# The bias of the last gate quarter moves from TensorE to VectorE in a quantised feed-forward stage

## What is computed

```python
def bit_linear(x, w, b):
    gamma_x = clip(max(abs(x), axis=-1), 1e-5)
    x_dq = clip(round(x * 127 / gamma_x), -128, 127) * gamma_x / 127
    gamma_w = clip(mean(abs(w)), 1e-5)
    w_dq = clip(round(w / gamma_w), -1, 1) * gamma_w
    return x_dq @ w_dq.T + b

gate = silu(bit_linear(x, gate_w, gate_b))     # 512 -> 2048
val = bit_linear(x, val_w, val_b)              # 512 -> 2048
x = x + bit_linear(gate * val, out_w, out_b)   # 2048 -> 512
```

## Time and profile before

| | us |
|---|---|
| median of 3 runs | 1772.95 |
| lowest and highest of them | 1772.92, 1774.59 |
| the profiled execution | 1772.19 |
| its span, first to last instruction | 1770.1 |
| the feed-forward stage in it | about 410 to 612 |
| granted TensorE clock, mean | 0.992 |

### The profile page before, as it was taken

One profiled execution on the slowest core, in us unless ns is written; L12 is line 12 of the kernel. 1 busy time (PEld: TensorE's weight loads), 2 busy tenths in 40 slices (PEclk: granted clock), 3 DMA queues, 4 the chain that ended last, 5 costly groups with the idle time before them and its releaser, 6 DMA issues. The chain is left out here.

```text
span 1770.1 us, 26445 instructions
## 1 busy us (share of the span) xinstructions
PE 1703.5 (96%) x9562; PEld 1391.0 (79%) x9582; DVE 1236.8 (70%) x2327; ACT 926.4 (52%) x1774; POOL 575.5 (33%) x455
## 2 busy tenths in 40 slices
PE   7999998997999979999999999999899999999998
PEld 6998997883444568888888788878777899999876
DVE  5444443796888768888788788888768576767555
ACT  4443332665565566666576667666331365656311
POOL 3111143014677532222222312121210355556332
PEclk9999999998999989999999999999999999999999
DMA  9323210963234671122222212110152579798563
GB/s 320 93 87 99 81 49 6 315 233 101 60 72 95 164 233 61 61 84 84 101 74 91 84 61 84 60 61 1 72 231 89 187 247 301 254 299 259 189 236 107
DMA packets 175563, 238.24 MB, mean 135 GB/s; under 512 B 51270, under 2 KB 112454, under 8 KB 173254
## 3 DMA queue, kind: packets, MB, share of 16 engines
q1 hardware_dynamic: 156620, 203.14, 35.1%
q0 software_dynamic: 9600, 33.30, 6.0%
q10 hardware_dynamic: 9216, 0.14, 0.3%
HBM read 184.24 MB, written 43.78 MB: 129 GB/s over the span
## 5 line engine op out<-in xcount | busy, mean ns | idle before, releaser
L1232 POOL TENSOR_TENSOR a_rq<-a_ssq,a_qhalf 128x4 f32<-128x4 f32 x64 | 65.6, 1025 | 358.8 <-DMA a_ssq<-a_sum_row 358.8
L78 PE MATMUL bank<-a_xT_hi,a_wq_lo 128*128 128x512 f32 (+1 forms) x384 | 144.3, 376 | 1.4 <-DVE a_xT_lo L503 1.4
L80 PE MATMUL bank<-a_xT_hi,a_wq_hi 128*128 128x512 f32 (+1 forms) x384 | 138.9, 362 | 0.0
L79 PE MATMUL bank<-a_xT_lo,a_wq_hi 128*128 128x512 f32 (+1 forms) x384 | 138.2, 360 | 0.0
L78 PE MATMUL bank<-a_wo_hi,a_oT_lo 128*128 128x512 f32 x320 | 127.3, 398 | 5.9 <-POOL a_wo_lo L1245 4.2
L1395 ACT ACTIVATE a_scores<-a_scores,a_nmax 128x256 f32<-128x256 f32 x256 | 126.9, 513 | 0.8 <-DVE a_nmax L1572 0.8
L80 PE MATMUL bank<-a_wo_hi,a_oT_hi 128*128 128x512 f32 x320 | 125.7, 393 | 0.0
L79 PE MATMUL bank<-a_wo_lo,a_oT_hi 128*128 128x512 f32 x320 | 125.7, 393 | 0.0
L2122 POOL TENSOR_TENSOR e_wg_lo<-raw_g,e_wg_hi 128x1408 fp32r<-128x1408 f32 x25 | 88.0, 3518 | 112.3 <-ACT e_wg_hi L2194 112.3
L1384 ACT ACTIVATE a_sum_row<-bank,a_sum_eps 1x512 f32<-1x512 f32 x64 | 43.4, 678 | 142.1 <-PE bank L1764 141.9
L1272 POOL TENSOR_TENSOR f_h<-f_vv,f_gs 128x512 f32<-128x512 f32 x64 | 92.8, 1454 | 61.4 <-DVE f_vv L1502 60.7
(11 more groups left out here) (423 smaller groups left out, 5380.1 us busy)
## 6 DMA issues: line engine op xcount, KB each, us to landing
raw_g<-in_egw SPq DMA_DIRECT2D x26, 704.0 KB, 4.5
raw_u<-in_euw SPq DMA_DIRECT2D x26, 704.0 KB, 6.0
a_xT_hi<-x1T_hi SPq DMA_DIRECT2D x16, 1024.0 KB, 6.2
a_xT_lo<-x1T_lo SPq DMA_DIRECT2D x16, 1024.0 KB, 8.3
raw_d<-in_edw SPq DMA_DIRECT2D x26, 512.0 KB, 3.9
y_routed<-m_y SPq DMA_DIRECT2D x39, 256.0 KB
raw_d<-in_edw SPq DMA_DIRECT2D x26, 192.0 KB, 4.4
a_cTraw<-in_ctxT SPq DMA_DIRECT2D x8, 512.0 KB, 5.7
```

What stands on the lines that cost most here:

```text
L78: pe.matmul(out, w[1], x[0], start=first, stop=False)
L79: pe.matmul(out, w[0], x[1], start=False, stop=False)
L80: return pe.matmul(out, w[0], x[0], start=False, stop=last)
L1232: pool.tensor_tensor(rq[:, h % HG, :], ssq[u % 2][:], qhalf[:], ALU.pow).then_inc(s_rq, 1)
```

## The change

For the last quarter of each tile (`j == NH - 1`) the bias product of TensorE is left out, and the first gate product opens the accumulation. VectorE takes the quarter out of its bank, scales it and adds the bias, in one instruction (`gate_biased`) that stands ahead of `val(n, 3)`, and writes it into `gs`. ScalarE then applies its function in place on `gs`, with no scale. The bias of this quarter, 512 numbers spread over 128 partitions (256 KB), is loaded once at the start of the stage, in front of the other transfers of SyncE. Two semaphores are new. The other three quarters are as before.

```diff
+        bg = sb("gate_bias", [P, 512])
...
+            sp.dma_start(bg[:], gate_bias_dram[H - 512:H].partition_broadcast(P)).then_inc(s_bg, 16)
             sp.dma_start(ahead.raw[:], wq_dram[:, :, 0:D]).then_inc(s_raw, 16)
...
             def silu(t, j):
                 u = t * NH + j
+                if j == NH - 1:
+                    act.wait_ge(s_gb, t + 1)
+                    act.activation(gs[u % 2][:], gs[u % 2][:], ACT.Silu).then_inc(s_gs, 1)
+                    return
                 act.wait_ge(s_g, u + 1)
...
+            def gate_biased(t):
+                u = t * NH + NH - 1
+                dve.wait_ge(s_g, u + 1)
+                dve.wait_ge(s_h, u - 1)
+                dve.scalar_tensor_tensor(gs[u % 2][:], gb[u % 2][:], sg[:, t:t + 1], bg[:], ALU.mult,
+                                         ALU.add).then_inc(s_gb, 1)
...
                     quantised_x(n + 3)
+                if n == 0:
+                    dve.wait_ge(s_bg, 16)
+                gate_biased(n)
                 val(n, 3)
...
-                    pe.matmul(gb[u % 2][:], rT[t % 3][:], gb6[:, cols], start=True, stop=False)
+                    if j < NH - 1:
+                        pe.matmul(gb[u % 2][:], rT[t % 3][:], gb6[:, cols], start=True, stop=False)
                     for c in range(KD):
-                        last = pe.matmul(gb[u % 2][:], xqT[t % 3][:, c, :], wg[:, c, cols], start=False, stop=c == KD - 1)
+                        last = pe.matmul(gb[u % 2][:], xqT[t % 3][:, c, :], wg[:, c, cols], start=c == 0 and j == NH - 1,
+                                         stop=c == KD - 1)
```

More of the change, by code:

```diff
@@ L1010, in ffn0_attention1 @@
 def ffn0_attention1(nc, banks, X, eps, ident, ones, limit, W, keep, prep, stored, rstd, x1T_dram, ahead, first, oT1,
-                    wq_dram, wo_dram, mask_dram, bq_dram, k_dram, v_dram, last, last_drams, B, S, G):
+                    wq_dram, wo_dram, mask_dram, bq_dram, k_dram, v_dram, last, last_drams, gate_bias_dram, B, S, G):
     T = B * S // P
@@ L1102, in ffn0_attention1 @@
         s_g, s_gs, s_v, s_vv, s_h = (sem(n) for n in ("gate", "silu", "val", "val_biased", "h"))
+        s_bg, s_gb = sem("gate_bias_loaded"), sem("gate_biased")
         s_half, s_ah, s_qh, s_sh, s_so, s_hr, s_hq = (sem(n) for n in (
@@ L2881, in program @@
                             k_dram, v_dram, last, (ktile(a["egw"][E]), ktile(a["euw"][E]), ktile(a["rwT"]), a["sdb"], a["egb"],
-                                                   a["eub"]), B, S, G)
+                                                   a["eub"]), a["gb"], B, S, G)
         if stop >= 4:
```

## The result

The changed kernel takes 1777.87 us (median of 10 runs, 1776.21 to 1783.17) against 1772.82 us for the kernel before (10 runs, 1770.14 to 1774.59). The ratio is 1.0032, with an interval of 1.0025 to 1.0040: 5.7 us slower (4.4 to 7.1). A second set of runs of the same kernel gave 1.0032 again (1.0021 to 1.0042). The prediction was 7.7 us slower, in a range that reaches from 2 to 13.

The account below looks back on a forecast made before the run. VectorE's loop with GpSimd and ScalarE was taken to bound most of the stage: sixteen rounds of 0.74 us, 11.8, less 4.1 absorbed, give 7.7 us on 1772.95, so 1780.7 us, range 1775.0 to 1786.0.

Parts of the forecast that it names:

- Who sets the pace: In most rounds VectorE's loop with GpSimd and ScalarE, not TensorE, whose sixteen removed products are worth 3.4 us if it bounds.
- the lag: Start of VectorE's last value quarter less start of TensorE's `down` products, same round; above some 3.5 us VectorE sets the pace.
- The rule from the Trainium skill: Improve the engine of highest occupancy: TensorE is the bound, so removing its products gives 3.4 us, 1769.5 us; chance 0.07.
- The step: VectorE's added instruction ahead of the last value quarter, 0.66 us each, sixteen times, 10.6 us in all.
- the 0.08 for ScalarE: Charge per round for ScalarE's later in-place function and its slower hand-over to GpSimd, 0.08 us (bounds 0 and 0.25).
- What absorbs: VectorE's waits for TensorE after round 0, nine of them, vanish when VectorE is late and take up 4.1 us.
- The reason that the prediction gave for the late rounds: In rounds 12 to 15 both paces are almost equal, VectorE 12.0 us and TensorE 11.8, so VectorE does not wait again.
- The sum: VectorE's last value quarter comes 11.8 - 4.1 = 7.7 us later, and attention starts later by the whole.
- the load: The 256 KB bias load at the stage's start takes 5.7 us, arrives before its first use and costs zero.
- One sign that was missed: The last value quarter of rounds 7 to 9 should move by 5 to 7 us, or the prediction is wrong.
- The passage into attention: At the stage's end TensorE is 5.5 to 6 us later with a lag near 3, and nothing is left to hide 2 us.
- ScalarE late: Its in-place function lasts 0.81 us or more and delays the norm and TensorE's `next_xT`; 11 us slower, 1784; chance 0.12.

Follow-up runs that it names:

- experiments 1: The changed kernel, but TensorE keeps its sixteen bias products of the last quarter; 1.0048 against the kernel before, 1.0035 when run again.
- 2: The kernel before, with the sixteen bias products of the last quarter left out and nothing in their place; 0.9990 against the kernel before.
- 5: The changed kernel with VectorE's new bias instruction done twice, the second over the first; 1.0104 against the kernel before.

## Why the prediction was right, point by point

**Who sets the pace: right.** The reading that rested on the waits and the lag held against the busy shares: 16 products removed from an engine that is 96% busy gave 1.5 us alone and 0.3 to 0.7 with the step there (experiments 1, 2), and a second step cost nearly in full (5). The rule from the Trainium skill, "Perfetto Trace Analysis", section "Identifying the Most-Contended Engine", which I had as a rival, named the wrong engine here when read by busy time alone: the edit takes work off the engine of highest occupancy, and the kernel is 5.7 us slower. The page's own warning is not to judge TensorE by that share but by its matmul throughput or its weight loads. Weight loads are busy 89.39 of 202 us in the stage, 44% against VectorE's 79%, so by that share the page does not point at TensorE.

**The step: 0.66 right, the 0.08 for ScalarE too much.** The rounds 0, 1, 2 and 4 to 11 grew by 0.66 to 0.73 us, 0.70 in the mean, not 0.74. Sixteen of them are 11.2 us, not 11.8. The in-place function lasts 0.63 us, under the 0.65 that I took and over the 0.61 estimated from the Trainium skill, "ScalarE: Activation LUTs", section "What ACT_TABLE_LOAD costs".

**What absorbs: right in place, small in size.** Rounds 3 and 12 to 15 took part of it up. From one last value quarter to the next, before and after:

| round | 3 | 12 | 13 | 14 | 15 |
|---|---|---|---|---|---|
| before | 13.11 | 12.02 | 11.64 | 12.13 | 11.66 |
| after | 13.00 | 11.93 | 11.43 | 11.42 | 11.44 |

They became 1.3 us shorter in place of 3.5 longer, which makes 4.85 absorbed, not 4.1. The waits alone are 4.1. What I left out is that a wait also breaks the overlap of two instructions: the next starts 0.65 us after a value quarter that lasts 0.74, but after a wait it starts only once the wait is over. That is some 0.09 us for each of nine waits. In the rows of after VectorE no longer waits in rounds 12 to 15, as the prediction asked. Its two waits left, both in round 0, are 2.9 us.

The reason that the prediction gave for the late rounds was only half right, though. It took both paces to be nearly equal there, 12.0 us for VectorE and 11.8 for TensorE. From tile 13 on there is no quantised input left to make, and VectorE's rounds 13 to 15 last 11.43 us, while the `down` products of rounds 12 to 14 stand 11.93 apart. So VectorE wins back 0.5 us in each of rounds 13 and 14, and the lag falls from 3.46 us in rounds 11 and 12 to 2.45 in round 14. It did not come to wait again because the lag was long enough for the few rounds left, not because the paces were equal.

**The sum.** 11.2 - 4.85 = 6.35 us at the last value quarter, and 6.5 at the stage's end, instead of 7.7. The timed 5.7 (4.4 to 7.1) agrees. The stated range, 2 to 13 us slower, is wide enough to hold almost any slower result, so these rows are the better test. Of the miss, 0.6 is the growth of a round and 0.75 the absorption. By the first measure the stage grew by only 5.5, because the second value quarter of round 0 came a microsecond earlier (8.04 us after the stage's start, where it was 9.05). Two executions of one kernel differ by 0.8 us there, with the clock's return, and in after the clock was back sooner than in before, as said above.

**The hand-over, and the load.** I had charged 0.08 us for ScalarE's part, and the rows show 0.05 (1.43 for 1.38). The load landed 5.6 us after its issue and nobody waited for it, as said.

**One sign that was missed.** The prediction wanted the last quarter of rounds 7 to 9 to move by 5 to 7 us. Counted from the second value quarter it moved by 4.8, 5.4 and 6.1, so round 7 falls just short: seven rounds grew by 0.70 each up to there, and round 3 shrank by 0.1.

**The passage into attention: right.** TensorE is 4.9 us later at its `down` of round 15, counted from the second value quarter (612.39 - 420.51 against 605.40 - 418.46; I had said 5.5 to 6), with a lag of 614.84 - 612.39 = 2.45 us (said: near 3, before: 1.05). Then it waits 1.20 us for the norm (`624.44`), and nothing is hidden: from the last value quarter to the last `next_xT` it is 30.5 us before and 30.7 after. The two belong together: 4.9 + 2.45 - 1.05 is the 6.35 of the sum.

**ScalarE late: a rival that was half there.** TensorE came to wait for ScalarE at two new places: 2.70 us in round 2 for the in-place step, which sets the gate bank free, and 2.60 us at the start of round 8 for the norm that stands behind it. I see no cost of its own in that: TensorE waits there for the same late VectorE, at another place, and rounds 2 and 8, which have these stalls, grow by 0.73 and 0.66 us like the others.

## What to carry to other kernels

Where two engines take turns in being late, read the lag between them at the same point of each round: it tells whose pace a round has, and the busy share does not. Before work is put into an idle time, ask whether what ends the idle time waits for that work; the same step cost 0.48, 0.71 and 1.38 us in three places of round 10. And before an instruction is moved out of a loop, look whether a blocked one behind it will simply fill its place; moving the blocked one gained where moving the other did not.

## What the runs showed of the hardware

A VectorE instruction on a single column took 0.12 to 1.14 us, according to how long GpSimd's product still ran beside it, and that product took 1.27 us alone and 2.18 under VectorE's 2048 columns. The in-place function took 630 ns from SBUF and 597 ns from a bank, 667 ns from a bank with a scale of each token. After its pause of 4.1 us TensorE's clock came back to the higher level at different times in two executions of one kernel, and the second value quarter came 0.8 us apart in them.
